# A wait between consecutive gathers: each of 5,312 indirect gathers on GpSimd waits until the one before it is reported done

## What is computed

```
Wg = codebook[idx_gate].reshape(2752, 1024)     # likewise Wu from idx_up; Wd from idx_down, (1024, 2752)
x = layernorm(x + attention(x, wq, wk, wv, wo))
y = (silu(x @ Wg.T) * (x @ Wu.T)) @ Wd.T
out = layernorm(x + y)
```

## Time and profile before

| | |
|---|---|
| Median of 3 runs | 13552.54 us (13550.04 to 13555.17) |
| Span of the profiled execution | 13555.1 us |
| POOL busy | 5592.7 us in 5,316 instructions |
| PE busy / weight loads | 7807.1 us / 4545.7 us, 29,072 each |
| DVE busy / ACT busy | 4989.8 us / 3676.3 us |
| Mean granted clock of PE | 0.727 of 2.4 GHz |

### The profile page before, as it was taken

The page is one execution under the profiler, slowest core; times in us unless marked ns, Lnnn a source line. Parts: engine busy times, 40 slices in busy tenths (PEclk is TensorE's granted clock), DMA queues, the critical chain, the costliest instruction groups (busy, mean ns, idle before and its releaser), DMA issues. The chain is left out here.

```text
span 13555.1 us, 109335 instructions
## 1 busy us (share of the span) xinstructions
PE 7807.1 (58%) x29072; PEld 4545.7 (34%) x29072; DVE 4989.8 (37%) x11788; ACT 3676.3 (27%) x6498; POOL 5592.7 (41%) x5316
## 2 busy tenths in 40 slices
PE   4333333333320100010001999999999999999999
PEld 1111111111100000000000666656666666666665
DVE  1000000000000000000000777777878787777875
ACT  0000000000000000000000776555555555555553
POOL 7777777777777777777776000000000000000000
PEclk6555555555555555555555999999999999999999
DMA  2011101111110000000000112222222222222221
GB/s 63 13 16 16 16 14 28 16 13 13 13 13 8 8 6 8 7 7 8 7 8 5 28 27 68 72 57 62 65 61 65 64 62 64 62 65 61 65 61 52
DMA packets 472442, 462.10 MB, mean 34 GB/s; under 512 B 231120, under 2 KB 347728, under 8 KB 467536
## 3 DMA queue, kind: packets, MB, share of 16 engines
q10 hardware_dynamic: 287072, 396.73, 10.4%
q0 software_dynamic: 169984, 22.10, 3.7%
q1 hardware_dynamic: 14832, 36.84, 0.7%
HBM read 398.07 MB, written 57.15 MB: 34 GB/s over the span
## 5 line engine op out<-in xcount | busy, mean ns | idle before, releaser
L203 POOL DMA_INDIRECT raw<-in_codebook_dram,idx_sb x5312 | 5592.5, 1053 | 1825.3 <-issue 1822.2
L413 PE MATMUL ps<-onehot,table 128*128 128x512 f32 x11776 | 3120.5, 416 | 68.8 <-DVE picked L987 48.3
L979 DVE TENSOR_SCALAR_CACHE_REDUCE onehot<-arena,small 128x512 fp32r<-128x512 f32 x3685 | 2514.6, 742 | 914.9 <-PE ps L413 900.1
L413 PEld LDWEIGHTS ps<-onehot,table 128*128 128x128 f32 x11776 | 2196.0, 188 | 912.2 <-issue 373.1
L272 PE MATMUL ps<-big,arena 128*128 128x512 f32 x1024 | 959.4, 958 | 1609.1 <-issue 1593.1
L745 ACT ACTIVATE onehot<-arena,small 128x512 fp32r<-128x512 f32 x2211 | 1434.9, 713 | 1208.4 <-PE ps L413 1130.4
L749 ACT ACTIVATE onehot<-onehot,small 128x512 fp32r<-128x512 f32 x2211 | 1425.0, 708 | 0.0
L893 DVE TENSOR_REDUCE small<-ps 128x1 f32<-128x384 f32 (+7 forms) x512 | 376.3, 753 | 2608.9 <-remote 2378.4
L441 PE MATMUL ps<-big,arena 128*128 128x512 f32 (+1 forms) x2816 | 1281.2, 592 | 1.3 <-DVE big L971 1.3
L320 PE MATMUL ps<-id_sb,arena 128*128 128x128 f32 x2304 | 385.5, 301 | 1324.7 <-issue 1272.9
L619 ACT COPY arena<-ps 128x512 f32<-128x512 f32 (+3 forms) x768 | 335.2, 484 | 2950.3 <-remote 2039.8
(11 more groups left out here) (70 smaller groups left out, 4227.3 us busy)
## 6 DMA issues: line engine op xcount, KB each, us to landing
arena<-code_low ACTq DMA_DIRECT2D x738, 256.0 KB, 3.4
arena<-code_high ACTq DMA_DIRECT2D x738, 128.0 KB, 3.3
raw<-in_codebook_dram,idx_sb POOLq DMA_INDIRECT x5312
gathered_units<-raw SPq DMA_DIRECT2D x40, 512.0 KB
arena<-gathered_units ACTq DMA_DIRECT2D x20, 1024.0 KB, 6.6
queries_keys<-arena ACTq DMA_DIRECT2D x16, 1024.0 KB
arena<-queries_keys ACTq DMA_DIRECT2D x32, 512.0 KB
big<-in_xT_dram ACTq DMA_DIRECT2D x4, 2048.0 KB, 19.4
```

The source lines that it names most:

```text
L203: pool.indirect_dma_start(raw[:, s, n, :], None, codebook, bass.IndirectOffsetOnAxis(ap=idx_sb[:, s, n:n + 1], axis=0),).then_inc(gathered ...
L413: last = mm(ps[:, bank + c, :], table[:, k, c, :], onehot[:, k, :], start=(k == 0), stop=(k == KLO - 1))
L979: dve.tensor_scalar(onehot[:, k, :], lo_sb[:, s % 2, :], kp_sb[:, k:k + 1], None, ALU.is_equal, ALU.add, accum_out=hits[:, k:k + 1]).then_ ...
```

## The change

A semaphore, `described`, is added. Each gather raises it by 1 through `engine_sem`, when GpSimd has finished the gather's instruction. That is when its transfers are described and handed over, which is apart from `gathered`, raised by the data's landing. Ahead of each gather but the first stands a wait until `described` has counted all the gathers before it, and an increment of `pool_passed`, which nothing waits for. In the loops the threshold of the wait is computed from the loop's counter.

```diff
+        described = sem("described"); unit_ready = sem("unit_ready")
...
-            def gather_unit(c, s, cols, loads, stores):
+            def gather_unit(c, s, cols, loads, stores, before):
                 pool.wait_ge(idx_in[s], loads)
                 past(pool, stored[s], stores)
                 pool.sem_inc(pool_passed, 1)
                 for n in range(cols):
+                    past(pool, described, before + n)
+                    pool.sem_inc(pool_passed, 1)
                     pool.indirect_dma_start(
                         raw[:, s, n, :], None, codebook,
                         bass.IndirectOffsetOnAxis(ap=idx_sb[:, s, n:n + 1], axis=0),
+                        engine_sem=described,
                     ).then_inc(gathered[c][s], 16)
...
-                        gather_unit(c, s, P, 16 * p + 16, 16 * p)
+                        gather_unit(c, s, P, 16 * p + 16, 16 * p, 2 * P * p + (s * P - P + CS * CS))
```

More of the change, by code:

```diff
@@ L153, in seq_post_ln_layer @@
         stored = [sem(f"stored{s}") for s in range(2)]
-        unit_ready = sem("unit_ready")
+        described = sem("described"); unit_ready = sem("unit_ready")
         prep_in = sem("prep_in"); prep_step = sem("prep_step"); lo_ready = sem("lo_ready"); lo_out = sem("lo_out")
@@ L205, in gather_unit @@
                         bass.IndirectOffsetOnAxis(ap=idx_sb[:, s, n:n + 1], axis=0),
+                        engine_sem=described,
                     ).then_inc(gathered[c][s], 16)
-            gather_unit(0, 0, CS * CS, 16, 0)
-            gather_unit(0, 1, P, 16, 0)
+            gather_unit(0, 0, CS * CS, 16, 0, 0)
+            gather_unit(0, 1, P, 16, 0, CS * CS)
             for c, (p0, p1) in enumerate(((1, PAIR_CUT), (PAIR_CUT, PAIRS + 1))):
@@ L212, in _ @@
                     for s in range(2):
-                        gather_unit(c, s, P, 16 * p + 16, 16 * p)
+                        gather_unit(c, s, P, 16 * p + 16, 16 * p, 2 * P * p + (s * P - P + CS * CS))
             for s in range(2):
-                gather_unit(1, s, P, 16 * PAIRS + 32, 16 * PAIRS + 16)
+                gather_unit(1, s, P, 16 * PAIRS + 32, 16 * PAIRS + 16, 2 * P * (PAIRS + 1) + (s * P - P + CS * CS))
         @block.sync
```

## The result

| | before | changed |
| --- | --- | --- |
| Median (lowest to highest) | 13553.85 us (13550.04 to 13556.78) | 9604.38 us (9598.1 to 9617.28) |
| Ratio, 95% interval | 1 | 0.709 (0.708 to 0.710) |
| Span of the profiled execution | 13555.1 us | 9615.1 us |

The change takes 29% off the time. The forecast was 7,790 us: the direction is right, and the measured time lies 1,814 us above it.

What follows compares the result with a forecast made beforehand. PE was taken to be held by the gather stream up to 7418 us, then to bound the kernel itself. First gather at 3.56 us, 5,311 pitches of 1.45 us (7,701 us) and the tail gave 7,790 us; range 6,900 to 12,700 us.

Steps and rivals of the forecast that it cites:

- The bound and its nature: Up to 7418 us the gather stream bounds the kernel by holding PE to its pace; after 7444 us PE itself does.
- the hold: PE kept to the gathers' pace, one PE instruction per gather, 1.40 us apart, until 26 us after the last gather.
- floor: Time PE needs once free: start, projections, attention and last stage, summing to 6,921 us.
- The backlog: Gathers put in ahead and not yet reported hold PE; with at most one unreported, PE goes free.
- What is late next: In the feed-forward stage PE waits for gathered units, the stream becoming the bound; PE's busy share falls to some 80%.
- The pitch: Time from one gather to the next under the wait: 1.45 us, bounds 1.25 and 2.09 us, 5,311 times.
- added register instruction: The one per gather in the loops, done while the gather before it runs, so it costs nothing.
- The tail: After the last pitch: 0.94 us gather, 1.5 us landing, 77.1 us to the end, 6 us for PE's lower clock.
- B: Rival: each gather itself holds PE, still one instruction per gather; 13,840 us at 1.45 us pitch, chance 0.14.
- C: Rival: the wait passes in the existing 0.30 us between gathers and PE stays held; 13,555 us, chance 0.04.
- D: Rival: PE gets n instructions per gather; 13,010 us with n = 4, 9,940 us with n = 8, chance 0.08.
- E: Rival: DVE's one-hots delay gathers in the last stage, pitch 2.19 us there; 10,890 us, chance 0.08.

Runs made afterwards that it cites:

- e6: Changed kernel with the wait loosened so one gather may be put in ahead of the one at work, in a set with the hold: 13220.01 us, ratio 0.975.
- e12: Changed kernel with the wait only ahead of every second gather, in a set with the hold: 8277.78 us, ratio 0.611 to the kernel before.
- e4: Changed kernel without the wait, argument and counter kept, in a set without the hold: 6927.17 us, kernel before 6928.37 us.
- e1: Changed kernel with one gather allowed ahead of the one at work, in a set without the hold: 6927.95 us, kernel before 6928.37 us.
- e11: Changed kernel with one gather allowed ahead and 11 further counter instructions before each gather, in a set with the hold: 8810.92 us, ratio 0.650.
- e9: Changed kernel with no wait and 19 further counter instructions before each gather, in a set without the hold: 11403.11 us, kernel before 6925.85 us.

## Why the prediction was right, and where it was short

**The bound and its nature: right.** PE was held by the stream and not by its own work. With the hold gone, the stages took what the prediction had summed from the free stretches: line 391 begins at 1621.8 us (forecast 1,616), and the whole without hold and without wait is 6,928 us (floor 6,921). That a gather beside PE does not hold it by itself, read from the free matmuls at 38 us, is what all of the changed kernel's windows show. The backlog was pictured as gathers, in the plural, put in ahead; e6 shows that one is enough when it is never interrupted. Whether what lifts the hold is the empty queue or the slower pitch was not separated.

**What is late next: right.** The stream became the bound through the units, and PE waits for them. From 1621.8 us to the end PE is busy for 5,233 of 7,993 us, 65% (71% is its share of the whole span). The prediction said some 80%, at its shorter pitch; its own sum, 5,305 us of work in some 6,170 us, gives about 85%. At the measured pitch it gives 5,305 / 7,993 = 66%, so the mechanism was right here and the number loose.

**The pitch: the term that was mis-sized.** The prediction took 1.45 us between bounds of 1.25 and 2.09 us; it measured 1.794 us, and the pitches came to 9,530 us in place of 7,701 us. These 1,829 us are the whole miss. With the measured pitch the sum is 3.6 + 9,530 + 0.95 + 1.4 + 78.9 = 9,615 us, the span of the profiled execution. The wrong step is the sentence "It is nearer to the lower end because the 0.30 us already hold the start of an instruction". The runs show 0.30 us only where the next gather had been put in while the preceding one ran (the kernel before, e6, and the second gather of a pair in e12). After a wait for the report it is 0.81 us, where the prediction had 0.51 us. No row of the kernel before could give this: the 0.85 us of idle time at 5017.88 us comes close, but it stands in the middle of a unit, where there was no wait. That the bounds took in the true pitch was therefore partly luck. The steady pitch of 1.75 us explains 5,311 x 0.30 = 1,593 us of the miss.

Another 5,311 x 0.044 = 234 us are breaks like that at 4024.98 us. The prediction had called the added register instruction free, and that holds. It stands only in the loops, from unit 2 on, and the steady pitch is 1.75 us in unit 0 as it is at 600 us, in the loop:

```profile
5.47 0.95 POOL L205 DMA_INDIRECT raw<-in_codebook_dram,idx_sb  x1 [0.82 <-DMA raw<-in_codebook_dram,idx_sb]
7.22 0.95 POOL L205 DMA_INDIRECT raw<-in_codebook_dram,idx_sb  x1 [0.81 <-DMA raw<-in_codebook_dram,idx_sb]
```

Most of the breaks are there without it as well: in e4, which has neither wait nor register instruction, the mean pitch is 0.032 us above the steady 1.249 us, 170 us in all. The prediction left them out of its pitch. Their cause is open.

**The other terms.** The tail: forecast 0.94 + 1.5 + 77.1 + 6 = 85.5 us, measured 0.95 + 1.4 + 78.9 = 81.3 us. Of the 6 us for the lower clock 1.8 us came.

**The rivals.** B (the hold stays, 15,670 us at the measured pitch) and C (13,555 us) are refuted by the time and by 35 PE instructions per gather. D (part of the hold goes) is refuted for the change, but e6 is just such a case: 2.7 instructions per gather. E (one-hots hold up the gathers) is refuted: from 7000 to 9000 us, beside the one-hots, 1,122 gathers took 1060.92 us, 0.95 us each.

```profile
7000.00:9000.00 2000.00, 984.50 (x3472) 649.37 (x3472) 768.97 (x1835) 552.21 (x881) 1060.92 (x1122) 0.75 0.18 36
```

The Trainium skill (SBUF — State Buffer, Who interferes with whom) lists `tensor_scalar` among the DVE operations that can enter a mode in which they lock GpSimd out, "not the form that also writes out its accumulator". DVE's one-hots are that form, so by that rule they should leave the gathers alone, and the trace agrees. The row at 32.45 us does not show a lock by itself, as the prediction has it; it shows a gather of 3.06 us beside DVE's preparation of the table.

**What no step foresaw.** All rows came from a trace with the hold. The kernel before was held in four sets; the change was timed in two of them, a gain in both. In the two sets without the hold the kernel before takes 6,926 to 6,928 us by itself. By the worked-out 9,600 us the forecast would have been wrong in sign there. That the result was taken in a set with the hold was luck.

## What to carry to other kernels

When an engine runs at one instruction per instruction of another engine, look for a stretch in which both run together freely. If there is one, the work doesn't collide by itself and some state may build up, so a pause may clear it. Here a pause after every second gather cost half of one after each (1.541 - 1.281 = 0.26 us per gather, against 0.51 us). A wait for the preceding instruction on the same engine exposes the start of the next one (0.81 us here), so don't price it by the gap of a stream that runs (0.30 us). And time the kernel before again beside every comparison, in every set: here the wait before every second gather takes 39% off in one set and adds 19% in another.

## What was not expected of the hardware

- The same kernel took 13,552 to 13,555 us in four sets and 6,926 to 6,928 us in two, with nothing between. The results number the chips; number 1 is found on both sides (6,928 us with e1 to e4, 13,554 us with e11 and e12). What differs between the sets is open.
- The hold reaches GpSimd's and SyncE's own instructions: 1,084 us of GpSimd's time in e6 lie in semaphore instructions of over 0.1 us, of which e1, the same kernel in a set without the hold, has none.
- Where the hold exists, a single gather of lead gives it: PE at 2.7 instructions per gather in e6, against 35 in the changed kernel's attention. With a pause of 0.80 us after every second gather it is gone but for attention's 400 us.
- Waiting for a gather's report before the next is put in costs 0.50 us on top of the 0.30 us between gathers (e12, side by side), while a wait that has already passed costs less than 0.01 us (1.286 against 1.281 us in e1 and e4).
- Twenty counter instructions ahead of a gather stretch its pitch to 2.13 us (e9). GpSimd's counters are thus no free filler: 2.130 - 1.281 = 0.85 us of pitch for the 19 added, 45 ns each. In the trace they start 78 ns apart, so part of them passes while a gather runs.
